# Message stage of a graph layer: two alternating edge banks, the turning and selecting of a part put behind the next part, and the second item's row gathers behind parts of the first

## The reference

```
x = x + message(layernorm(x), edge_attr, ...)        # x: 625 x 512, 20000 edges x 512, sorted by dst
x = x + experts(layernorm(x))                        # 64 experts, top 6, plus 2 shared ones

def message(xn, e, coef, src, dst, path):            # 512 = 16 segments x 32
    x1, x2 = xn[src].reshape(-1, 16, 32), e.reshape(-1, 16, 32)
    i1, i2, i3 = path[:, 0], path[:, 1], path[:, 2]  # 64 paths
    contrib = coef[None, :, None] * x1[:, i1, :] * x2[:, i2, :]
    edge_out = zeros(20000, 16, 32).at[:, i3, :].add(contrib)
    return zeros(625, 512).at[dst].add(edge_out.reshape(-1, 512))

def experts(h):
    gate = top-6 of softmax(h @ Wr), normalized
    shared = sum over 2 of silu(h @ sWg) * (h @ sWu) @ sWd
    routed = sum over 64 of (silu(h @ Wg) * (h @ Wu) @ Wd) * gate
    return shared + routed + h
```

## Time and profile before

| | us |
|---|---|
| median of three runs | 1120.15 |
| lowest, highest | 1119.8, 1122.91 |
| span of the profiled execution (first to last instruction, the only time the profile has of it) | 1129.7 |
| VectorE busy | 562.6 |
| TensorE busy | 917.5 |
| first products of the message stage | 44.36 |
| last contraction of the message stage starts | 494.34 |

### The profile page before, as it was taken

The page is one execution under the profiler, slowest core; times in us unless marked ns, Lnnn a source line. Parts: engine busy times, 40 slices in busy tenths (PEclk is TensorE's granted clock), DMA queues, the critical chain, the costliest instruction groups (busy, mean ns, idle before and its releaser), DMA issues.

```text
span 1129.7 us, 20307 instructions
## 1 busy us (share of the span) xinstructions
PE 917.5 (81%) x7194; PEld 497.2 (44%) x7195; DVE 562.6 (50%) x1321; ACT 227.2 (20%) x579; POOL 345.8 (31%) x390
## 2 busy tenths in 40 slices
PE   0156775777757767769999999999997999999988
PEld 0023333334333333337645454454543645446355
DVE  5368889889798898977621111112111111111116
ACT  1021321313222123114111111112111121121110
POOL 3715243252342534001232323223232232332220
PEclk9978898987899899999999999999998999999999
DMA  8835465464644655557699999999999999999918
GB/s 244 288 128 187 164 202 196 148 220 161 218 159 143 224 192 180 187 189 255 239 385 390 389 395 391 394 393 392 394 391 395 390 390 393 395 386 396 399 67 320
DMA packets 70341, 321.04 MB, mean 284 GB/s; under 512 B 12879, under 2 KB 13032, under 8 KB 48315
## 3 DMA queue, kind: packets, MB, share of 16 engines
q1 hardware_dynamic: 48021, 260.82, 60.7%
q0 software_dynamic: 21248, 56.55, 15.4%
q10 hardware_dynamic: 934, 1.80, 0.6%
HBM read 308.55 MB, written 13.62 MB: 285 GB/s over the span
## 4 chain that ended last, share of the span: by engine, by line
PE 64%; DVE 10%; issue 8%; another core or an unknown queue 7%; DVEq 5%; ACT 2%; DMA 0%
PE ps L1222 20%; PE ps L1268 10%; PE ps L615 8%; DVE big L596 7%; PE ps L848 6%; PE ps L1166 4%; PE ps L666 3%; PE ps L875 3%; PE ps L650 2%; DVEq L587 2%; DVEq L594 2%; PE ps L1215 2%; PE ps L1242 1%; PE ps L634 1%
## 5 line engine op out<-in xcount | busy, mean ns | idle before, releaser
L596 DVE TENSOR_TENSOR big<-big 128x512 f32 (+1 forms) x640 | 384.7, 679 | 80.4 <-remote 37.9
L615 PE MATMUL ps<-big,mixed 128*32 128x256 f32 x2512 | 181.3, 416 | 92.0 <-issue 48.2
L1222 PE MATMUL ps<-big 128*64 128x512 f32 x1024 | 240.0, 612 | 14.2 <-issue 14.2
L333 POOL DMA_INDIRECT big<-xn_d,idx x157 | 166.0, 1057 | 268.4 <-DVE big L596 207.8
L1127 POOL DMA_INDIRECT big<-h_d,idx x64 | 63.0, 984 | 359.8 <-issue 276.7
L615 PEld LDWEIGHTS ps<-big,mixed 128*32 128x32 f32 x2512 | 82.9, 118 | 184.6 <-issue 86.3
L1232 DVE TENSOR_TENSOR mixed<-big,ps 128x256 f32<-128x256 f32 x64 | 27.0, 421 | 271.1 <-ACT big L1229 270.7
L1222 PEld LDWEIGHTS ps<-big 128*64 128x64 f32 x1024 | 69.3, 139 | 139.7 <-issue 134.0
L1268 PE MATMUL ps<-big,mixed 128*64 128x256 f32 x1024 | 124.6, 385 | 0.1
L1183 POOL DMA_INDIRECT y_d<-big,sia x74 | 75.3, 1017 | 123.4 <-DVE big L1281 73.7
L625 ACT ACTIVATE mixed<-ps 128x512 f32<-128x512 f32 x40 | 23.9, 597 | 319.1 <-PE ps L615 264.8
(11 more groups left out here) (212 smaller groups left out, 673.1 us busy)
## 6 DMA issues: line engine op xcount, KB each, us to landing
big<-in_L_ffn_Wg SPq DMA_DIRECT2D x64, 1024.0 KB
big<-in_L_ffn_Wu SPq DMA_DIRECT2D x64, 1024.0 KB
big<-in_L_ffn_Wd SPq DMA_DIRECT2D x64, 1024.0 KB
big<-in_edge_attr SPq DMA_DIRECT2D x39, 1024.0 KB
big<-y_d SPq DMA_DIRECT2D x10, 768.0 KB, 12.1
big<-xn_d,idx POOLq DMA_INDIRECT x157
big<-in_L_ffn_sWg SPq DMA_DIRECT2D x2, 1024.0 KB, 5.0
big<-in_L_ffn_sWu SPq DMA_DIRECT2D x2, 1024.0 KB, 7.1
```

The source lines that it names most:

```text
L333: pool.indirect_dma_start(xs[s][:, c, :], None, xn_d[:, :], bass.IndirectOffsetOnAxis(ap=table[:, c0 + c:c0 + c + 1], axis=0)).then_inc(x_ ...
L596: ins = dve.tensor_tensor(pr[k % 2][:, 0:chunks, EXT * p:EXT * (p + 1)], xs[s][:, 0:chunks, ds(o1, EXT)], es[s][:, 0:chunks, ds(o2, EXT)], ...
L615: ins = pe.matmul(bank(BA)[WIN * h:WIN * (h + 1), h0:h0 + HP * EXT], onehot[s][:, CW * h + r, :], pr[k % 2][:, CW * h + r, :], start=r == ...
L1222: ins = pe.matmul(bank(k2)[TA * h:TA * (h + 1), :].rearrange("p (w f) -> p w f", w=2), xgT[k2][:, k, 0:TA], gu[:, :, k, W * h:W * (h + 1)] ...
```

## The change

The two banks `BA` and `BT_` become a pair that alternates by quarter (`edge_bank`). A quarter is contracted into one of them, evicted, turned back into the same bank, and evicted from there, while the next quarter is contracted into the other. The contraction's wait on `ev_ok` for the quarter before becomes a wait on `evt_ok` for the second eviction of the quarter before that.

The order of the calls is now by part. After the contraction of an even part stands the turning of the quarter before and its second eviction; after that of an odd part the selection of the quarter before, then the first eviction of the present quarter. The last quarter of an item is turned and selected in the next item's parts 0 and 1, and the sums are evicted there. The puts are spread one block to a part (parts 2 to 6), the one-hot columns four to a part (parts 2 to 5), and the placement comes at part 7.

The gathers of item 1 are now issued with the waits that later items have: three at once, then threes behind parts 0, 1, 2 and 3 of item 0, the last behind part 4.

The counts on which VectorE waits for the message sum are constants now instead of register values; for that the loops for wider windows were rewritten so that they leave the banks empty. Two waits at the kernel's end are constants as well.

```diff
@@ gather_sources
-            if until is not None and c % PER == 0:
+            if until is not None and c % PER == 0 and (c > 0 or not at(until, 0)):
                 pool.wait_ge(part_ok, until + c // PER)
@@
     gather_sources(0, idx, 0, chunks=EC0)
-    gather_sources(1, idx, EC)
@@
-    BA, BT_, BS, BM = 0, 1, 2, 3
+    BA, BS, BM = 0, 2, 3
+
+    def edge_bank(qq):
+
+        return bank(BA + qq % 2)
@@ one_hots
-        for c in range(chunks):
+        for c in range(c0, min(c1, chunks)):
             ins = act.activation(onehot[s][:, c, :], iotaw[:, 0:WIN], ACT.Abs, bias=bias(c))
+        if c1 < chunks:
+            return
@@ contract
-        if k % 2 == 0 and (k > 0 or not at(t, 0)):
-            pe.wait_ge(ev_ok, PARTS * t + k // 2)
+        if k % 2 == 0 and (k > 2 or not at(t, 0)):
+            pe.wait_ge(evt_ok, PARTS * t + k // 2 - 1)
@@
-                ins = pe.matmul(bank(BA)[WIN * h:WIN * (h + 1), h0:h0 + HP * EXT], onehot[s][:, CW * h + r, :],
-                                pr[k % 2][:, CW * h + r, :], start=r == 0,
+                ins = pe.matmul(edge_bank(k // 2)[WIN * h:WIN * (h + 1), h0:h0 + HP * EXT],
+                                onehot[s][:, CW * h + r, :], pr[k % 2][:, CW * h + r, :], start=r == 0,
@@ turn
         pe.wait_ge(ev_ok, PARTS * t + qq + 1)
-        if qq > 0 or not at(t, 0):
-            pe.wait_ge(evt_ok, PARTS * t + qq)
         for f in range(FPP):
-            ins = pe.transpose(bank(BT_)[:, P * f:P * (f + 1)], ev[:, P * f:P * (f + 1)], ident[:, :])
+            ins = pe.transpose(edge_bank(qq)[:, P * f:P * (f + 1)], ev[:, P * f:P * (f + 1)], ident[:, :])
@@ the loop over items
         if 0 < t < NG - 1:
             load_edges(1 - s, SHORT + t * GE, SUB * t)
+        if t < NG - 1:
             gather_sources(1 - s, idx, EC * (t + 1), SUB * t)
         chunks = EC if t else EC0
         products(t, s, 16 * QW * (t // 2 + 1), 16 * EC * (t // 2) + 16 * (EC if s else EC0), chunks)
-        for qq in range(PARTS):
-            contract(t, s, 2 * qq, chunks)
-            contract(t, s, 2 * qq + 1, chunks)
-            evict(t, qq)
-            turn(t, qq)
-            evict_turned(t, qq)
-            select(t, qq)
-            if t > 0 and qq < 2:
-                put(t - 1, range(3) if qq == 0 else range(3, NB), start=t == 1)
-            if qq == 1 and t + 1 < NG:
-                one_hots(t + 1, 1 - s, lambda c: wdst[:, EC * (t + 1) + c:EC * (t + 1) + c + 1])
-            if qq == 2:
+        for k in range(SUB):
+            contract(t, s, k, chunks)
+            q = PARTS * t + k // 2 - 1
+            if q >= 0 and k % 2 == 0:
+                turn(q // PARTS, q % PARTS)
+                evict_turned(q // PARTS, q % PARTS)
+            if q >= 0 and k % 2 == 1:
+                select(q // PARTS, q % PARTS)
+            if k % 2 == 1:
+                evict(t, k // 2)
+            if t > 0 and k == 1:
+                evict_sums(t - 1)
+            if t > 0 and 2 <= k < 2 + NB:
+                put(t - 1, range(k - 2, k - 1), start=t == 1)
+            if t + 1 < NG and 2 <= k < 6:
+                one_hots(t + 1, 1 - s, lambda c: wdst[:, EC * (t + 1) + c:EC * (t + 1) + c + 1],
+                         CW * (k - 2), CW * (k - 1))
+            if k == SUB - 1:
                 place_rows(t, nrow[:, t:t + 1])
-        evict_sums(t)
+    turn(NG - 1, PARTS - 1)
+    evict_turned(NG - 1, PARTS - 1)
+    select(NG - 1, PARTS - 1)
+    evict_sums(NG - 1)
     put(NG - 1, range(NB), stop=True)
@@ more_item and its loop (skipped in the profile): sums added behind each item, banks set to zero at the end
...
@@ add_messages
-        dve.wait_ge(put_ok, nput - (NB - 1 - b))
-        if b == 0:
-            dve.wait_ge(added_ok, nput - (NG * NB - 1))
+        dve.wait_ge(put_ok, NB * (NG - 1) + b + 1)
         VV(add_block(b))
```

More of the change, by code:

```diff
@@ L265, in sem, with at @@
         return nc.alloc_semaphore(name)
+    def at(t, *of):
+        return isinstance(t, int) and t in of
     class Count:
@@ L314, in gnn_moe @@
     x_in = [sem(f"x_in{k}") for k in (0, 1)]
+    part_ok = sem("part_ok")
     def load_edges(s, first, until=None, quarters=range(QW), short=False):
@@ L557, in gnn_moe, with one_hots @@
     regs = [[dve.alloc_register(f"off{k}_{m}") for m in range(2 * HP)] for k in (0, 1)]
-    BA, BT_, BS, BM = 0, 1, 2, 3
-    def at(t, *of):
-        return isinstance(t, int) and t in of
-    def one_hots(t, s, bias, chunks=EC):
-        if not at(t, 0, 1):
+    BA, BS, BM = 0, 2, 3
+    def edge_bank(qq):
+        return bank(BA + qq % 2)
+    def one_hots(t, s, bias, c0=0, c1=EC, chunks=EC):
+        if c0 == 0 and not at(t, 0, 1):
             act.wait_ge(part_used, SUB * t - SUB)
-        for c in range(chunks):
+        for c in range(c0, min(c1, chunks)):
             ins = act.activation(onehot[s][:, c, :], iotaw[:, 0:WIN], ACT.Abs, bias=bias(c))
+        if c1 < chunks:
+            return
         ins.then_inc(oh_ab, 1)
@@ L625, in evict @@
         act.activation(ev.rearrange("p (u q) -> p u q", q=PP),
-                       bank(BA).rearrange("p (q u) -> p u q", q=PP), ACT.Copy).then_inc(ev_ok, 1)
+                       edge_bank(qq).rearrange("p (q u) -> p u q", q=PP), ACT.Copy).then_inc(ev_ok, 1)
     def turn(t, qq):
         pe.wait_ge(ev_ok, PARTS * t + qq + 1)
-        if qq > 0 or not at(t, 0):
-            pe.wait_ge(evt_ok, PARTS * t + qq)
         for f in range(FPP):
-            ins = pe.transpose(bank(BT_)[:, P * f:P * (f + 1)], ev[:, P * f:P * (f + 1)], ident[:, :])
+            ins = pe.transpose(edge_bank(qq)[:, P * f:P * (f + 1)], ev[:, P * f:P * (f + 1)], ident[:, :])
         ins.then_inc(tp_ok, 1)
@@ L641, in evict_turned @@
             act.wait_ge(sel_ok, PARTS * t + qq)
-        act.activation(evT, bank(BT_), ACT.Copy).then_inc(evt_ok, 1)
+        act.activation(evT, edge_bank(qq), ACT.Copy).then_inc(evt_ok, 1)
     def select(t, qq):
@@ L745, in more_item @@
         gather_sources(1, idxx, 0, chunks=chunks)
-        dve.wait_ge(put_ok, NB * t)
-        dve.wait_ge(added_ok, NB * x + 1)
-        for b in range(NB):
-            add_block(b).then_inc(added_ok, 1)
+        dve.wait_ge(added_ok, NB * x + NB + 1)
         dve.tensor_scalar(wdx[:, :], wdst[:, ds(c0, EC)], woff[:, ds(j + 1, 1)], None, ALU.add)
@@ L767, in more_item @@
         put(t, range(NB), start=True, stop=True)
+        dve.wait_ge(put_ok, NB * t + NB)
+        for b in range(NB):
+            add_block(b).then_inc(added_ok, 1)
+    none_left = sem("none_left")
     with nc.If(nmax > 0):
+        dve.wait_ge(put_ok, NB * NG)
+        for b in range(NB):
+            add_block(b).then_inc(added_ok, 1)
         with nc.Fori(0, nmax) as j:
@@ L776, in gnn_moe @@
                 more_item(j, g, first, EC)
-    nput = nmax * (NG * NB) + NG * NB
+        for b in range(NB):
+            dve.memset(bank(BM + b), 0.0).then_inc(none_left, 1)
+        dve.wait_ge(none_left, NB)
     nparts = nmax * (NG * SUB) + NG * SUB
```

9 lines of the change are left out of this document (4 added, 5 removed).

## The result

| | kernel before | changed kernel |
|---|---|---|
| median of the runs | 1121.53 us (1119.8 to 1126.93, 4 runs) | 1066.55 us (1065.9 to 1068.3, 4 runs) |
| span of the profiled execution | 1129.7 us | 1067.1 us |

The direction was right and the size was wrong. The experiments then showed something larger: most of the gain exists only in some sessions on the chip.

A forecast was written before the change was run, and what follows sets the result against it. VectorE was taken to pace the message stage, transfers the expert stage; gains of 27 + 5 + 9 − 1 = 40 us in the profiled execution, times 0.9, gave 36 us and 1084 us, range 1068 to 1104.

The forecast's parts named there:

- The end: From last contraction to first sum: selection and placement added ahead of the sums, 1 us lost, bounds 0 and 2.
- The factor from the profiled execution to the runs: Profiled span is 9.5 us above the runs' median, so the 40 us gain was scaled by 0.9 to 36.
- Rival 1: Item 0's stop stays because full rings, not the unbroken gather run, hold TensorE: 1092 us; chance 0.20.
- rival 2: Message stage: TensorE becomes the bound under gathers, parts 1 to 4 taking 5.4 and 5.9 us: 1101 us; chance 0.10.
- rival 4: Message stage slower: TensorE granted only 1.2 GHz, 48.0 us an item against 44.9: 1139 us; chance 0.04.
- rival 5: No change: the gain is waited away in the transfer-bound expert stage: 1120 us; chance 0.03.
- (B): Seven waits at part 2, items 1 and 3 to 8, 19.9 us, contraction held under gathers: 5 gained, bounds 0 and 15.
- rival 3: The part 2 waits go too, as TensorE has less behind it when six gathers come: 1070 us; chance 0.13.
- (C): Ten waits, mostly at part 4, 31.9 us, from turning, selection and puts before the next contraction: 27 gained, bounds 16 and 32.
- (A): One 13.21 us wait in item 0, TensorE held until transfers end; spaced gathers gain 9, bounds 0 and 13.2.
- the 40 of the sum: Total gain forecast for the profiled execution, 27 + 5 + 9 − 1 us, a span of 1089.7 us.
- the 65.0 us: VectorE's waits before products, 51.8 in items 1 to 9 and 13.2 in item 0: most the message stage could give.

The follow-up runs named there:

- e6: Changed kernel with old order, old banks and item 1's gathers in one piece, constant counts kept; late session: 1120.88 us, ratio 0.9976 to the kernel before.
- e1: Changed kernel with old order and old banks, item 1's gathers still spread; prompt session: 1065.78 us, ratio 0.9994 to the kernel before.
- e3: Changed kernel with the old order of calls, two alternating banks and spread gathers kept; prompt session: 1068.79 us, ratio 1.0004 to the kernel before.
- e5: Changed kernel unaltered, run again in a late session on chip 14: 1065.72 us, ratio 0.9495 to the kernel before.
- f2: Changed kernel with new order and two banks, item 1's gathers in one piece; prompt session on chip 7: ratio 0.9969 to the kernel before.
- i1: Changed kernel unaltered, in a prompt session on chip 15: 1064.96 us, ratio 0.9972 to the kernel before.
- i2: Changed kernel with item 1's gathers in one piece, prompt session on chip 15: ratio 0.9965 to the kernel before.
- e4: Changed kernel with old order and banks, item 1's gathers spread, row gathers of items 2 to 9 left out; prompt session: 1071.01 us, ratio 1.0047.
- f4: Old order and banks, item 1's gathers spread, row gathers of items 2 to 9 left out; prompt session on chip 7: ratio 1.0054 to the kernel before.

## Why the prediction was wrong

**What held.** VectorE was the pace-maker and the waits before its products were what could be had. The expert stage passed the gain on. The end cost 1.55 us, inside its bounds of 0 and 2, in part by luck: 0.7 are the order's, the rest is the half clock of that execution. The factor from the profiled execution to the runs was 55.0/62.6 = 0.88, forecast as 0.9. Rivals 1, 2, 4 and 5 did not come: no wait in item 0, none at parts 3 to 5, a clock of 0.973, a gain that reached the end.

**The step that failed** is "(B) is not reached by the order". I gave (B) 5 of its 19.9 us, with 15 as the upper bound. Since nothing but 2.6 us is left, all of it at part 2, 17.3 were gained, more than that bound. That is rival 3, to which I gave 0.13, and its number, 1070, was the nearest. The argument rested on one contraction that starts promptly and was held under the same gathers. In the changed kernel it still starts promptly and is still held, but VectorE goes on 5.25 us after its start (80.29 to 85.54) instead of 6.68 (95.31 to 101.99). With a start 0.15 us earlier against VectorE's products that makes the 1.58 us by which the wait fell, 1.92 to 0.34. One difference is that before, a selection ended right ahead of it, and now TensorE stands for 1.89 us there. Whether this is why was not tried. Nor is a wait at part 2 as steady as I took it: e6, in the old order and a late session, has some 9 us at part 2 and 37 elsewhere, so the split of the gain between (B) and (C) is that of one execution.

**The other terms of the sum** were all sized too low: (C) 31.9 us gained for 27, (A) 13.2 for 9, and 1.4 us at the start of the stage (first product 42.92) for nothing. 17.3 + 31.9 + 13.2 + 1.4 − 1.55 = 62.3, beside a span shorter by 62.6. Against the 40 of the sum, (B) makes 12.3 us of the difference, (C) 4.9 and (A) 4.2. For both (A) and (C) I kept back a residue because a hold might outlast the slack of a part; it never did.

**The cause that I gave for (C) was wrong in part.** I read the earlier trace rows as a chain of turning, selection and puts that is too long for a part. That chain is whole in e1, e3 and the kernel before in prompt sessions, and VectorE waits 3.0 us in e1 and 5.8 in e3. In the earlier trace rows it is too long because the contraction ahead of it and the one behind it end late, 1.81 + 1.41 us, and because its puts ran at a granted clock of 0.62, 1.69 us more; TensorE had stood for 2.53 and 0.69 us ahead of them. The stops and the low clock go together: from 66 to 380 us the clock is 0.88 in the kernel before and 0.89 in e6, 0.95 in the changed kernel and e5, 0.97 in e1. I had kept late ends for (A) and (B); e6 against e1 says that late ends and the clock behind them make nearly all of the 65.0 us. One profile shows this only to who looks for "remote" on ScalarE and for the clock under the puts.

**A row misread.** The 3.8 us that I took for one contraction under three gathers are two contractions, 64 matmuls in 3.79 us, and ScalarE waited for both. The first released VectorE after 3.34 us. So the 3.8 in rival 2, in the odd parts and in the estimate for (A) was 0.5 us too long.

**A rule weighed.** I set the Trainium skill, SBUF — State Buffer, section "Who interferes with whom", against the earlier trace rows: "DMA never contends with a compute engine". f2 and i1 agree with it: TensorE and the same transfers run side by side. In the late session's profile the eviction of 85.38 starts 3.23 us after its turning, on a release tied to no instruction, where 0.69 is what i1 has. Even there transfers without an indirect DMA beside them go with prompt ends (157 of 157 signals from 505 to 1030 us). What the traces hold against the rule is only the late ends beside indirect DMAs in two sessions of eight, and they don't say that these are a contention. Rival 1's full rings alone are not enough either.

**What stays open.** What makes a session late (not the chip's number, not the change, and not the clock, which differs by kernel within one). Which of order, second bank and spread gathers a late session needs: all kernels that part them met prompt sessions. Only their sum is measured there (0.9495 and 0.9515). In prompt sessions they are told apart: the new order with its two banks is worth 0.3 to 0.4% in each of five (0.9962 to 0.9972, every interval below 1), the second bank nothing (0.9997 to 1.0016 over five), the spread gathers nothing on top of the order (i1 0.9972, i2 0.9965). That the gathers make the ends late was to be tried with e4 and f4, which met prompt sessions; in its place stands the count above, which shows that the two go together, not what leaving the gathers out would give. Why (B) went is open as well.

## What to carry to other kernels

A wait in one profile has a cause and an occasion; before costing a chain, measure the kernel before in a second session, since here its times were 55 us apart, and the same order waited 58 us in one (e6) and 3 in another (e1). Work put one part behind the engine that sets the pace costs little when all is prompt (here it gained 3 us) and absorbs lateness when it is not (2.5 us at the turning of 82.15). When such slack is there, count a wait that is shorter than it as gone but for a few tenths: of 51.8 us 2.6 were left here, all waits having been under 4.9.

## What was unexpected of the hardware

The kernel before has two times, 1116 to 1130 us in late sessions and 1062 to 1076 in prompt ones, of one kind within a session over up to 31 runs, with granted clocks of 0.94 to 0.96 and 0.97 to 0.99. In the late session of e5 and e6 ScalarE waits 104 and 74 us on releases that the trace ties to no instruction; in e1 and i1, of prompt sessions, none. Late ends of TensorE's work fall beside indirect DMAs of GpSimd (291 of 832 signals in the four late profiles) and hardly ever elsewhere (3 of 1228), at DMA shares of 0.37 and of 0.98 alike. The changed kernel takes 1064 to 1068 us in late sessions and 1061 to 1069 in the prompt one.
